# A gated attention and feed-forward kernel: the first tile's square root moves from ACT to POOL, as a power

## The reference

```
q = instance_norm(layernorm(x)); k = c = instance_norm(ctx); s = ctx
qp = Wq q + bq;  kp = Wk k + bk;  sp = Ws s + bs
attn    = softmax(qp^T kp)                        512 x 512 per sequence
mean    = attn sp;   mean_sq = attn (sp * sp)
std     = sqrt(relu(mean_sq - mean * mean))
x       = x + tanh(g_xattn) * (c * std + mean)
x       = x + tanh(g_ffn) * (layernorm(x) @ W.T)  W: 4-bit weights, scaled and shifted by group
```

## Time and profile before

| what | value |
|---|---|
| median of 2 runs | 185.67 us |
| the profiled execution | 186.42 us |
| its span (first to last instruction) | 184.6 us |
| mean granted clock of PE | 0.999 |
| PE busy | 167.2 us (91%), 1128 matmuls |
| PE's weight loads | 147.1 us (80%) |
| DVE busy | 141.0 us (76%) |
| ACT busy | 118.0 us (64%) |
| POOL busy | 120.4 us (65%) |
| chain that ended last, by engine | PE 76%, DVE 9%, ACT 4%, issue 4%, POOL 3%, DMA 2% |

### The profile page before, as it was taken

The page is one execution under the profiler, slowest core; times in us unless marked ns, Lnnn a source line. Parts: engine busy times, 40 slices in busy tenths (PEclk is TensorE's granted clock), DMA queues, the critical chain, the costliest instruction groups (busy, mean ns, idle before and its releaser), DMA issues.

```text
span 184.6 us, 3489 instructions
## 1 busy us (share of the span) xinstructions
PE 167.2 (91%) x1128; PEld 147.1 (80%) x1128; DVE 141.0 (76%) x311; ACT 118.0 (64%) x261; POOL 120.4 (65%) x145
## 2 busy tenths in 40 slices
PE   1554999999999999999999999999999979789992
PEld 0432889999999999999999999998789867567881
DVE  2897696689859887986988798676159679988851
ACT  2253575978598678859867885995569995232110
POOL 1455586917955896799589679944328959966310
PEclk9999999999999999999999999999999999999999
DMA  6408566883796699679679966356100000111212
GB/s 169 166 21 202 186 159 138 237 201 86 184 319 153 155 287 245 162 216 286 139 170 249 283 145 153 78 134 151 44 0 0 4 0 0 57 62 60 111 57 114
DMA packets 14321, 25.75 MB, mean 139 GB/s; under 512 B 2336, under 2 KB 2464, under 8 KB 14304
## 3 DMA queue, kind: packets, MB, share of 16 engines
q1 hardware_dynamic: 14304, 25.54, 52.2%
HBM read 9.67 MB, written 2.10 MB: 64 GB/s over the span
## 4 chain that ended last, share of the span: by engine, by line
PE 76%; DVE 9%; ACT 4%; issue 4%; POOL 3%; DMA 2%; SPq 0%; ACTq 0%; POOLq 0%
PE pv_bank L322 28%; PE turn_bank L306 14%; PE score_bank L296 8%; PE score_bank L297 8%; PE side_bank L333 3%; PE score_bank L377 3%; PE score_bank L371 3%; PE score_bank L370 3%; DVE X L667 2%; DMA CTX<-in_context 2%; PE side_bank L342 2%; ACT probs L442 1%; PE side_bank L283 1%; DVE result L692 1%; DVE stats L673 1%
## 5 line engine op out<-in xcount | busy, mean ns | idle before, releaser
L831 POOL TENSOR_SCALAR probs<-probs,rden 128x512 f32<-128x512 f32 x64 | 50.9, 796 | 32.2 <-DVE rden L623 32.0
L322 PE MATMUL pv_bank<-probs_t,values 128*128 128x128 f32 x512 | 67.7, 276 | 0.0
L442 ACT ACTIVATE probs<-score_bank,neg_max 128x512 f32<-128x512 f32 x64 | 44.1, 690 | 31.4 <-DVE neg_max L616 30.8
L322 PEld LDWEIGHTS pv_bank<-probs_t,values 128*128 128x128 f32 x512 | 62.4, 192 | 2.1 <-issue 1.7
L616 DVE TENSOR_REDUCE neg_max<-score_bank 128x1 f32<-128x512 f32 x64 | 43.5, 682 | 15.0 <-PE score_bank L297 14.4
L306 PE MATMUL turn_bank<-ident,probs 128*128 128x128 f32 x256 | 38.8, 275 | 1.1 <-ACT probs_t L450 1.0
L450 ACT COPY probs_t<-turn_bank 128x512 f32<-128x512 f32 x64 | 37.1, 581 | 3.2 <-PE turn_bank L306 3.0
L306 PEld LDWEIGHTS turn_bank<-ident,probs 128*128 128x128 f32 x256 | 31.1, 142 | 5.7 <-POOL probs L831 1.1
L296 PE MATMUL score_bank<-c_both,q_both 128*128 128x512 f32 x64 | 29.3, 458 | 2.3 <-ACT q_with_x L494 2.3
L297 PE MATMUL score_bank<-c_with_bias,q_with_x 128*128 128x512 f32 x64 | 26.4, 412 | 0.0
L296 PEld LDWEIGHTS score_bank<-c_both,q_both 128*128 128x128 f32 x64 | 13.0, 202 | 4.6 <-issue 2.9
(11 more groups left out here) (99 smaller groups left out, 243.6 us busy)
## 6 DMA issues: line engine op xcount, KB each, us to landing
c_both<-c_hi SPq DMA_DIRECT2D x30, 128.0 KB, 2.6
X<-in_x SPq DMA_DIRECT2D x8, 256.0 KB, 3.0
CTX<-in_context SPq DMA_DIRECT2D x8, 256.0 KB, 4.1
ctx_now<-in_context SPq DMA_DIRECT2D x8, 256.0 KB, 2.9
sz<-in_scales_zeros SPq DMA_DIRECT2D x4, 512.0 KB, 6.7
out<-result SPq DMA_DIRECT2D x8, 256.0 KB, 2.0
q_with_x<-x_hi SPq DMA_DIRECT2D x15, 128.0 KB, 2.3
c_with_bias<-c_lo SPq DMA_DIRECT2D x15, 128.0 KB, 2.9
```

What stands on the lines that cost most here:

```text
L322: last = pe.matmul(pv_bank[b][:, P * j:P * j + P], values[t % 2][:, i, b, :, :].rearrange("p a c -> p (a c)"), probs_t[g % PROBS_T][:, P * ...
L442: act.activation(probs[g % PROBS][:, :], score_bank[g % SBANKS][:, :], ACT.Exp, bias=neg_max[:, c:c + 1], accum_out=den[:, c:c + 1]).then_ ...
L831: pool.tensor_scalar(probs[g % PROBS][:, :], probs[g % PROBS][:, :], rden[:, c:c + 1], 1.0, ALU.mult, ALU.mult).then_inc(probs_done, 1)
```

## The change

The root of tile 0's variance is no longer an activation on ACT. POOL computes it as VAR ** 0.5 with one TENSOR_TENSOR instruction of 128x512, whose second input is a column of 0.5 that is broadcast along the row. The instruction stands in chunk 4 of tile 6, behind the relu of tile 5 and ahead of the normalisation of chunk 54, and raises `first_root_done`. DVE's product and sum for tile 0 wait for that semaphore and move from chunk 7 to chunk 4 of tile 7. On ACT root 1 takes the place that root 0 had, and the call of root 1 behind the loop goes. The counts of `root_done` shift by one. The column of 0.5 is a memset of POOL in its prologue, ahead of `split_x_lo(1)`.

```diff
--- before.py
+++ after.py
@@ -91,6 +91,7 @@
         averages = sb("averages", [P, P])
         power = sb("power", [P, 2])
         tanh_g = sb("tanh_g", [P, 2])
+        half = sb("half", [P, 1])
 
         w_int = pair_of("w_int", [P, N], I32)
         sz = pair_of("sz", [P, 2, N])
@@ -173,6 +174,8 @@
         ffn_hi_done = sem("ffn_hi_done")
         ffn_lo_done = sem("ffn_lo_done")
         root_done = sem("root_done")
+        first_root_done = sem("first_root_done")
+        half_ready = sem("half_ready")
         scaled_done = sem("scaled_done")
         x2_done = sem("x2_done")
         stats2_done = sem("stats2_done")
@@ -501,7 +504,7 @@
                     if g + AHEAD_E < LAST:
                         exponentials(g + AHEAD_E)
                     elif c == 6:
-                        root(0)
+                        root(1)
                     if g > 0:
                         keep_turned(g - 1)
                     if c == 0 and t + 1 < TILES:
@@ -513,7 +516,6 @@
                     if t == TILES - 1 and 1 <= c <= 4:
                         weights_hi(c - 1)
 
-            root(1)
             keep_turned(LAST - 1)
             keep_xt_hi(0)
             root(2)
@@ -657,7 +659,7 @@
                 dve.tensor_tensor(w_deq[:, g, :], w_deq[:, g, :], side_bank[:, :], ALU.subtract).then_inc(w_centred, 1)
 
             def scale_first_context():
-                dve.wait_ge(root_done, 1)
+                dve.wait_ge(first_root_done, 1)
                 dve.tensor_tensor(CTX[:, 0, :], CTX[:, 0, :], VAR[:, 0, :], ALU.mult).then_inc(scaled_done, 1)
 
             def after_attention(u):
@@ -769,7 +771,7 @@
                     if t == TILES - 1:
                         if c < GROUPS:
                             centre_weights(c)
-                        if c == 7:
+                        if c == 4:
                             scale_first_context()
                             after_attention(0)
 
@@ -854,7 +856,7 @@
 
             def scale_context(u):
 
-                pool.wait_ge(root_done, u + 1)
+                pool.wait_ge(root_done, u)
                 if u == 1:
                     pool.wait_ge(scaled_done, 1)
                 pool.tensor_tensor(CTX[:, u, :], CTX[:, u, :], VAR[:, u, :], ALU.mult).then_inc(scaled_done, 1)
@@ -889,6 +891,7 @@
             split_c_lo(0)
             inverse_deviation(1)
             pool.memset(averages[:, :], 1.0 / N).then_inc(consts_ready, 1)
+            pool.memset(half[:, :], 0.5).then_inc(half_ready, 1)
             split_x_lo(1)
             for g in range(AHEAD_E):
                 normalise_probs(g)
@@ -905,6 +908,11 @@
                         inverse_deviation(t + 2)
                     if c == 4 and t > 0:
                         relu(t - 1)
+                    if c == 4 and t == TILES - 2:
+                        pool.wait_ge(half_ready, 1)
+                        pool.wait_ge(relu_done, 1)
+                        pool.tensor_tensor(VAR[:, 0, :], VAR[:, 0, :], half[:, :].broadcast_to([P, N]),
+                                           ALU.pow).then_inc(first_root_done, 1)
                     if c == 5 and t + 2 < TILES:
                         split_x_lo(t + 2)
                     if c == 6 and t + 1 < TILES:
```

## The result

The changed kernel takes 264.95 us in the median against 185.67, a ratio of 1.425 (95% interval 1.417 to 1.433): 79.3 us slower. It was forecast slower, at 253 with a range of 196 to 265; the median lies 0.05 us inside the upper end of that range. The profiled execution has a span of 263.4 us against 184.6, 78.8 more.

What follows compares the result with a forecast made beforehand. PE was taken to bound tile 6 and most of tile 7, DVE the tail. Stall 65.2, clock 2.6 and tail -0.65 make +67.2 us on the profiled 186.42, so 253.6, or 253 us for the median; range 196 to 265.

Steps and rivals of the forecast that it cites:

- The price of the power: POOL's new power in tile 6: 0.136 us per further column, so 70 us for 512 columns.
- The cover: Tile 6: a power on POOL of up to 4.9 us would not delay PE's transposes of chunk 54.
- Step 1: Tile 6: PE's transposes of chunk 54 start late behind the power and nothing is caught up, +65.2 us.
- Step 2: After the wait in tile 6: PE runs for a while at the 1.2 GHz level, +2.6 us.
- Step 3: ACT, end of tile 7: one root less, table load stays, copy 63 starts earlier; 0.5 us off ACT.
- Step 4: DVE, tile 7: earlier product and sum of tile 0 make PE's probabilities of 63 0.25 us late, hidden.
- Step 5: Tail after tile 7: root 1 ready earlier, DVE's full stretch and PE's behind it move by -0.65 us.
- The contention: Tail: POOL's long one-column powers, up to 1.007 us, lose time to DVE; undisturbed price 0.55 us.
- hidden: Rival: the power in tile 6 ends inside the 4.9 us cover, only the tail's gain is left, 185.0 us; chance 0.17.
- the loop overlaps partly: Rival: columns of a long power cost less, 23 us in all, kernel 206 us, 190 to 240; chance 0.22.

Runs made afterwards that it cites:

- e5: Kernel before the change plus a list of POOL powers of 1 to 64 columns and two products at the end of POOL's queue; one execution, 239.8 us.
- e4: Changed kernel with the power on only 64 of the 512 columns; ratio to the kernel before 1.0384.
- e8: Changed kernel with the power on only 128 of the 512 columns; ratio to the kernel before 1.0889.
- e10: Changed kernel with the power on only 32 of the 512 columns; ratio to the kernel before 0.9999.
- e2: Changed kernel with a product in place of the power and DVE's product and sum for tile 0 back in chunk 7; ratio to the kernel before 0.9943.
- e1: Changed kernel with an ordinary product of the same size and place instead of the power; ratio to the kernel before 0.9957.
- e7: Kernel before with roots 0 to 2 on ACT in tile 6's chunk 5, and second-step products, sums and statistics inside tile 7; ratio 0.9961.
- e6: Kernel before with root 0 on ACT in tile 6's chunk 5, root 1 in its old place, DVE's part in tile 7's chunk 4; ratio 0.9964.

## Why the prediction was right, and where its size was off

The direction and the mechanism were the ones forecast: POOL's queue holds the probabilities of 54 behind the power, PE waits, nothing is caught up, and the tail gains a little.

- **The price of the power**, the term that was mis-sized. Put at 70 us (0.136 a column) it measured 81.94 (0.160). The prediction subtracted L880's 0.563 from L812's 0.699 and multiplied by 510. e5 shows a clean first column at 0.549 and a second at 0.155 more: the rows used were 14 ns too high for one column and 5 too low for two, and 510 x 0.019 is 10 us. With the step's growth from 0.155 to 0.159 along the row (2 us more) that is the whole miss of 12 us. That L880, and not the two-column rows, was mostly off is shown; why it took 14 ns longer stays open. The upper pair of the prediction, 0.707 less 0.548, gave 159 ns and 82 us. It is partly luck that it hit: the clean rows give a step of 155 ns, and the 0.707 was 3 ns too high.
- **The cover**: 4.9 us forecast, 4.91 measured four times. **Step 1**: 65.2 became 77.2, which but for 0.2 us is the power's 11.8.
- **Step 2**, the clock: 2.6 forecast, 2.2 in the changed kernel, 2.4 and 2.9 in e4 and e8, none in e10. The 2.6 was read from the kernel's start in one execution, and that stretch isn't the same in each: the slow spacing lasts from 17.65 to about 23.3 in the kernel before, from 18.29 to about 21.8 in the changed kernel, and in e2 matmuls follow at 0.23 us from 18.09, then slowly until about 21.6. So that it came so near is partly luck.
- **Step 3**: as forecast, one root less (260 of ACT's instructions against 261) and the table load still there (225.75), copy 63 directly behind mean_sq.
- **Step 4**: the reciprocal of 63 comes 1.76 us behind that of 62 (224.07 to 225.83) where it was 1.23, so 0.5 late and not 1.0, as DVE's product took 0.67 there and no longer 1.43, and the sum behind it 1.06 instead of 0.75. POOL's last probabilities were 0.8 us late against PE's transposes of 62, and not 0.25: they start at 227.01, behind a product (L854) that took 1.70 us instead of 1.27, and end at 228.14, 0.15 us ahead of PE's transposes of 63. It cost nothing, as PE waits 0.90 for ACT's copy as before, but little of that cover was left; e2 shows that moving DVE's part was worth nothing either.
- **Step 5**: 0.65 forecast, 0.67 read in the trace, 0.8 (0.4 to 1.2) in e1's ratio. As forecast, POOL's product (229.34 to 230.61) was ready first and DVE's own order set the sum at 231.08.
- **The contention** on POOL's one-column powers was assumed and isn't shown. e5's one-column call, with DVE idle, takes 0.549, which fits; no run isolated it.

What the Trainium skill, GPSIMD Engine Reference, section "3.1 Elementwise — side-by-side cycle accounting", gives for a two-input operation fits L860, and e1's product of 1.04 us lies a little below the estimate of 1.1 us from it; read as a rule for the power it is off by some 70 times, as 0.159 us a column stands to 2.2 ns. With the measured terms the sum closes: 77.2 + 2.2 - 0.7 = 78.7 against the 78.8 of the spans. The rival "hidden" was right about the cover and the tail, and wrong on the price alone; "the loop overlaps partly" falls with the 81.94 us and with e5. Its 190 to 240 us is rounded: by the prediction's own terms powers of 9.3 to 60 us give 192 to 243, which changes nothing here. The measured median, 264.95, lies at the upper end of the range (265), since the range went down for that second rival and only 12 us up. That it lies inside by 0.05 us is luck; the bounds that the prediction gave for its own mechanism, 248 to 268, hold it with room.

## What to carry to other kernels

Here POOL's power costs 0.159 us for every column, short row or long: fine for one or two columns of deviations, ruinous on a tile (81.9 us for 512). When a price is extrapolated by hundreds from the difference of two short rows, an error of some 20 ns is an error of 10 us; let the range go as far up as the spread of both rows, times the columns, allows. And a slot in a queue has a cover that can be counted beforehand from who waits for the next instruction (here 4.9 us): what is put there was free up to it and paid in full beyond, with some 2 to 3 us for the clock on top where PE had stood for 5.6 us or more.

## What was not expected of the hardware

- A table load pair in the middle of the attention loop, 2.6 us on ACT, was free where PE bounds the stage (e6: 0.9964).
- PE's fall to the 1.2 GHz level cost 2.4, 2.9 and 2.2 us behind waits of 5.6, 15.8 and 77 us: nearly a fixed sum. There was none behind 0.52 us (e10), and in e7 the fall came behind a wait of only 2.10 us, 0.9 us after PE had started again. The granted clock shows these falls. At the start of the kernel before, by contrast, it reads 1.00 over matmuls spaced at 0.43 us, as this window shows (length, PE's busy us, granted clock, DMA); e2 has the fall there too, and its granted clock does show it, with 0.50 from 20.00 to 22.00.

```profile
16.00:23.00 7.00, 5.35 (x19) 1.00 0.67 191
```

- DVE's two-input sums can take more than twice their time beside POOL: 1.75 and 1.82 us in e7, while POOL's products and probabilities run, for what takes 0.75 in the earlier trace rows. POOL's product runs beside that 0.75 too and takes 1.71 us (the greatest of L860 in the earlier trace rows), so either engine can be the one that is slowed; no run shows what decides it.
